# Transposes of the second normalisation moved to the bank of probabilities times values, with their activations split over two steps

## What is computed

```python
x = x + tanh(g_xattn[0]) * xattn(layernorm(x), ctx, ctx, mask, Wq, bq, Wk, bk, Wv, bv)
x = x + tanh(g_ffn[0]) * ffn(layernorm(x), Wg, W1, W2, W3)
# xattn: softmax((q Wq + bq)(k Wk + bk)^T / sqrt(10), masked) (v Wv + bv), by head
# ffn:   scores = (x_flat @ Wg.T).T ; each of 8 experts takes its top n/8 tokens
#        y = (silu(xg W1) * (xg W3)) W2 * softmax(top scores), added back by token
```

## Time and profile before

| | us |
|---|---|
| median of 3 runs | 1004.09 |
| lowest, highest | 1002.74, 1007.72 |
| the profiled execution | 999.87 |
| its span | 998.1 |
| PE busy | 783.9 (79%) |
| DVE busy | 608.9 (61%) |
| ACT busy | 516.7 (52%) |
| POOL busy | 401.4 (40%) |

### The profile page before, as it was taken

The page is one execution under the profiler, slowest core; times in us unless marked ns, Lnnn a source line. Parts: engine busy times, 40 slices in busy tenths (PEclk is TensorE's granted clock), DMA queues, the critical chain, the costliest instruction groups (busy, mean ns, idle before and its releaser), DMA issues. The chain is left out here.

```text
span 998.1 us, 22875 instructions
## 1 busy us (share of the span) xinstructions
PE 783.9 (79%) x7244; PEld 615.0 (62%) x7244; DVE 608.9 (61%) x1501; ACT 516.7 (52%) x1002; POOL 401.4 (40%) x777
## 2 busy tenths in 40 slices
PE   3488888798889888987897721116899999999994
PEld 1366666566666665665666511112798899889884
DVE  1457777677667667766767618879545544644530
ACT  2356576657665666666566711000555665666551
POOL 3344334433443344334432132003355675575434
PEclk9799999999999899989999955555899999999997
DMA  3875558656866585667556235001154365453223
GB/s 116 233 202 129 162 173 237 172 167 178 227 156 180 159 220 148 186 185 184 155 144 159 71 94 186 0 1 44 44 109 119 72 128 113 109 92 47 55 33 42
DMA packets 99261, 130.60 MB, mean 131 GB/s; under 512 B 12896, under 2 KB 62336, under 8 KB 99200
## 3 DMA queue, kind: packets, MB, share of 16 engines
q1 hardware_dynamic: 86912, 112.78, 40.2%
q0 software_dynamic: 12288, 17.05, 10.5%
HBM read 52.34 MB, written 26.49 MB: 79 GB/s over the span
## 5 line engine op out<-in xcount | busy, mean ns | idle before, releaser
L684 DVE TENSOR_REDUCE m_sb<-a_ps 128x4 f32<-128x512 f32 x256 | 165.0, 676 | 17.5 <-PE a_ps L825 16.4
L541 ACT ACTIVATE p_t<-b_ps 128x512 f32<-128x512 f32 x256 | 147.6, 587 | 52.4 <-PE b_ps L838 50.3
L1351 POOL DMA_INDIRECT out<-y,idx_add x64 | 100.1, 1565 | 107.8 <-DVE idx_add L1451 71.6
L825 PE MATMUL a_ps<-k_st,q_st 97*128 97x128 bf16 x1024 | 100.2, 221 | 21.7 <-DMA k_st<-k_part 16.2
L1341 POOL DMA_INDIRECT xg<-rows_scratch,idx x64 | 67.7, 1058 | 103.6 <-issue 89.1
L455 POOL TENSOR_TENSOR q_part<-q_rest,q_part 128x512 bf16<-128x512 f32 x32 | 36.9, 1154 | 179.4 <-ACT q_part L512 179.4
L825 PEld LDWEIGHTS a_ps<-k_st,q_st 97*128 97x128 bf16 x1024 | 73.9, 98 | 55.4 <-issue 48.9
L838 PE MATMUL b_ps<-q_st,k_st 99*128 99x128 bf16 x1024 | 100.2, 221 | 4.7 <-ACT p_t L541 4.7
L1549 PE MATMUL bank<-x_hi,w_hi 128*128 128x512 f32 x256 | 100.7, 393 | 1.5 <-DVE x_lo L1477 1.5
L1549 PE MATMUL bank<-x_hi,w_lo 128*128 128x512 f32 x256 | 99.9, 390 | 0.0
L1549 PE MATMUL bank<-x_lo,w_hi 128*128 128x512 f32 x256 | 99.7, 390 | 0.0
(11 more groups left out here) (193 smaller groups left out, 1728.4 us busy)
## 6 DMA issues: line engine op xcount, KB each, us to landing
q_st<-q_part SPq DMA_DIRECT2D x96, 256.0 KB, 4.7
k_st<-k_part SPq DMA_DIRECT2D x96, 256.0 KB, 4.1
w<-in_w_t SPq DMA_DIRECT2D x24, 512.0 KB, 4.9
rows_scratch<-row SPq DMA_DIRECT2D x16, 528.0 KB, 4.1
x_in<-in_x SPq DMA_DIRECT2D x16, 512.0 KB, 4.9
c_t<-in_ctx_t SPq DMA_DIRECT2D x16, 512.0 KB, 4.9
x_res<-in_x SPq DMA_DIRECT2D x16, 512.0 KB, 3.7
out<-x SPq DMA_DIRECT2D x16, 512.0 KB, 3.3
```

What stands on the lines that cost most here:

```text
L541: act.activation(p_t[b.s % 2][:, 4 * q:4 * q + 4, :], b_ps[q % 2][:].rearrange("p (h s) -> p h s", s=P), ACT.Exp, scale=SCALE).then_inc(ex ...
L684: dve.tensor_reduce(m_sb[b.s % 2][:, 4 * q:4 * q + 4], a_ps[q % 2][:].rearrange("p (h s) -> p h s", s=P), AX_X, ALU.max).then_inc(max_done, 1)
L825: mm = pe.matmul(a_ps[q % 2][:, i * P:(i + 1) * P], q_st[g.p][0:A_K, h, tok], k_st[g.p][0:A_K, h, tok], start=True, stop=True)
L1351: pool.indirect_dma_start(out[:, :], bass.IndirectOffsetOnAxis(ap=idx_add[e.p][:, st:st + 1], axis=0), y[st][:], None, compute_op=ALU.add) ...
```

## The change

- `xn2_back` writes `pv_ps` instead of `o_ps`, half 0 in step 0 and half 1 in step 1, both for group g-3. It waits for the copy of `pv_ps` of batch b-4 (`pv_out`). `values` of that step waits for the copy of the half (`xt2_out`).
- `out_back` has `o_ps` for itself and waits for DVE's last use of it (`ot_out`) alone.
- `normalise2` makes two rows' activations in step 2 and two in step 3, where it made four in step 2.
- `router` and `router_out` are done in step 1 (from 0), `scores_back` and `row_scores` in step 2 (from 1), `store_scores` in step 3 (from 2). `store_rows` stays in step 3, and what it waits for is made a step later.

The diff:

```diff
--- before.py
+++ after.py
@@ -252,25 +252,6 @@
 
 
 
-    O_USES = sorted([((j, OT_AT), "ot", j) for j in range(GB)]
-                    + [((3, 0), "xt", 0), ((0, 0), "xt", 1)])
-    O_LAG = {("xt", 0): 2, ("xt", 1): 3}
-
-    def o_free(eng, g, q, j):
-
-        at = [x[0] for x in O_USES].index((j, q))
-        for back in range(1, 4 * len(O_USES)):
-            i, turn = (at - back) % len(O_USES), (at - back) // len(O_USES)
-            (_, what, n) = O_USES[i]
-            if what == "ot":
-                use = Batch(g.k, 4 * g.p + n + 4 * turn, NB).back(4)
-                if use.ok:
-                    return wait(eng, ot_out, use.times(1, 1))
-            else:
-                use = g.on(turn - O_LAG[what, n])
-                if use.ok:
-                    return wait(eng, xt2_out, use.times(2, n + 1))
-
     with nc.Block() as block:
 
         @block.sync
@@ -394,9 +375,9 @@
                 if b.j == 1:
                     store_x2(g.on(-2))
                 if b.j == 2:
-                    store_scores(g.on(-3))
                     stack_q(g.on(1))
                 if b.j == 3:
+                    store_scores(g.on(-3))
                     store_rows(g.on(-3))
                     stack_k(g.on(1))
                 max_rows(b.back(1))
@@ -565,7 +546,7 @@
                 if g.ok:
                     act.wait_ge(xt2_done, g.times(2, k + 1))
                     wait(act, r_done, g.times(1))
-                    act.activation(xn2_t[:, k, :], o_ps[:], ACT.Copy).then_inc(xt2_out, 1)
+                    act.activation(xn2_t[:, k, :], pv_ps[:], ACT.Copy).then_inc(xt2_out, 1)
 
             def router_out(g):
                 if g.ok:
@@ -599,10 +580,8 @@
                 if b.j == 2:
                     hi_k(f, 0)
                 neg_hi(b.back(1))
-                if b.j == 0:
-                    xt2_copy(g.on(-3), 1)
-                if b.j == 3:
-                    xt2_copy(g.on(-2), 0)
+                if b.j < 2:
+                    xt2_copy(g.on(-3), b.j)
                 if b.j == 2:
                     normalise2(g.on(-2), (0, 1))
                 if b.j == 3:
@@ -619,13 +598,13 @@
                     hi_q(f, 1)
                 if b.j == 2:
                     hi_k(f, 1)
-                if b.j == 2:
+                if b.j == 3:
                     normalise2(g.on(-2), (2, 3))
                 if b.j == 3:
                     normalise(g.on(2), (2, 3))
                 exp(b.back(2), 2)
                 pv_copy(b.back(3))
-                if b.j == 0:
+                if b.j == 1:
                     router_out(g.on(-3))
                 if b.j == 1:
                     mid_q(f, 1)
@@ -765,7 +744,7 @@
                 if b.j == 3:
                     make_v(f, 1)
                 maximum(b, 3)
-                if b.j == 1:
+                if b.j == 2:
                     row_scores(b.group.on(-3))
 
             steps(dve, step)
@@ -839,10 +818,12 @@
                                    start=True, stop=True)
                 mm.then_inc(b_done, 1)
 
-            def values(b, q):
+            def values(b, q, back):
                 if not b.ok:
                     return
                 if q == 0:
+                    if b.j in (1, 2) and back.ok:
+                        pe.wait_ge(xt2_out, back.times(2, b.j))
                     pe.wait_ge(f_free[1], b.group.times(4, 4))
                     pe.wait_ge(f_free[0], b.group.times(4, 4))
                     wait(pe, pv_out, b.times(1))
@@ -882,10 +863,10 @@
                 if use.ok:
                     if isinstance(use.k, int) and use.k + use.s == 0:
                         pe.wait_ge(f_free[1], 4)
-                    if b.j == 1 and g.ok:
+                    if b.j == 2 and g.ok:
                         pe.wait_ge(r_out, g.times(1, 1))
                         pe.sem_inc(passed, 1)
-                    if b.j == 2 and g.ok:
+                    if b.j == 3 and g.ok:
                         pe.wait_ge(st_out, g.times(1, 1))
                     wait(pe, nmid_done, use.times(1))
                     pe.wait_ge(max_done, use.times(4, 4))
@@ -894,18 +875,21 @@
             def out_back(b):
                 use = b.back(4)
                 if use.ok:
-                    o_free(pe, b.group, OT_AT, b.j)
+                    wait(pe, ot_out, use.times(1))
                     pe.wait_ge(pv_out, use.times(1, 1))
                     for a in range(4):
                         mm = pe.transpose(o_ps[:, a * P:(a + 1) * P], o_t[use.s % 2][:, a, :], ident[:])
                     mm.then_inc(ot_done, 1)
 
-            def xn2_back(g, k, at):
-                if g.ok:
-                    o_free(pe, *at)
+            def xn2_back(g, k, b):
+                if g.ok:
+                    last = b.back(4)
+                    pe.wait_ge(pv_out, last.times(1, 1) if last.ok else NB)
+                    if k == 1 and not b.back(3).ok:
+                        pe.wait_ge(xt2_out, g.times(2, 1))
                     pe.wait_ge(xn2_done, g.times(4, 4))
                     for t in range(GB):
-                        mm = pe.transpose(o_ps[:, t * P:(t + 1) * P], row[g.p][:, t, k * P:(k + 1) * P], ident[:])
+                        mm = pe.transpose(pv_ps[:, t * P:(t + 1) * P], row[g.p][:, t, k * P:(k + 1) * P], ident[:])
                     mm.then_inc(xt2_done, 1)
 
             for u in range(8):
@@ -923,19 +907,17 @@
                     scores_t_(*((b.back(2), q - 1) if q else (b.back(3), 3)))
                     if q == 2:
                         for i in range(4):
-                            values(b.back(3), i)
-                        if b.j == 0:
+                            values(b.back(3), i, g.on(-3))
+                        if b.j == 1:
                             router(g.on(-3), b)
-                        if b.j == 1:
+                        if b.j == 2:
                             scores_back(g.on(-3), b)
                     if q in (0, 2):
                         front(g.on(1), 2 * b.j + q // 2)
                     if q == 0:
                         max_t(b)
-                    if (b.j, q) == (3, 0):
-                        xn2_back(g.on(-2), 0, (g, q, b.j))
-                    if (b.j, q) == (0, 0):
-                        xn2_back(g.on(-3), 1, (g, q, b.j))
+                    if q == 0 and b.j < 2:
+                        xn2_back(g.on(-3), b.j, b)
 
             steps(pe, step)
 
```

## The result

The changed kernel is slower: 1012.10 us (median of 7 runs, 1006.65 to 1016.77) against 1004.09, a ratio of 1.0063 with a 95% interval of 1.0040 to 1.0086. The forecast was 1004.0 us, with 995 to 1012 as its range. The profiled execution took 1012.28 us, 12.4 more than that of before. Of these, 8.1 lie in the attention part. The other 4.3 us lie behind it, in code that the change doesn't touch. Over all the traces that part took 411.8 to 416.5 us, and both ends of that range are traces of the kernel before, so they are scatter.

What follows compares the result with a forecast made beforehand. It took POOL's chain and the transfers into `k_st` as the bound, not PE's step 3 waits. Terms 0 - 3.3 + 4.5 - 1.4 = -0.2 us against the profiled 999.87; by the median 1004, range 995 to 1012.

Steps and rivals of the forecast that it cites:

- 2 written-out ones: Written-out groups: the late store of the rows was to cost 0.5 us in each, as in full-clock groups.
- What bounds the kernel: Loop groups at full clock: POOL's chain and the last transfer into `k_st` set the end, not PE's step 3 waits.
- The naive 30 us: Step 3: both PE waits, 2.75 us in each of some 12 groups, counted as saved in full; the forecast rejected this.
- Step 3 at half clock, -3.3 us: Step 3: the 1.1 us gained is kept only in the three loop groups partly at half clock, -3.3 us.
- The moved pieces, 0: Stretch from first scores to last projection of q: moved transposes and router work cancel; 0, bounds -0.3 and +0.4 us a group.
- a wait of 0.2 to 0.3: Same stretch: PE's wait for the copy of half 1, 0.2 to 0.3 us, was to go out of it.
- The store, +4.5 us: Step 3: later store of the rows delays the pieces of k by 0.5 us in nine groups, +4.5 us.
- The clock, the rival at 0.17: First scores: longer PE idle drops the clock, 1.0 to 1.5 us a group, some 1011 us in half of them; chance 0.17.
- The drain, -1.4 us: Last batch: transposes into `o_ps` follow `values` by 1.7 us, not 3.2; -1.4 us, bounds -0.5 and -2.
- The rival of the bubbles: All 12 groups: `k_st` comes earlier along with step 3, so the 1.13 us stay; 989 us, chance 0.05.

Runs made afterwards that it cites:

- the bank alone: Kernel before with only the second normalisation's transposes moved from `o_ps` to `pv_ps`, same steps 3 and 0: 995.32 us, ratio 0.9939.
- the trace without it: Changed kernel with 64 semaphore increments that nobody waits for at the start of PE's program: single run 1006.92 us beside 1004.86.

## Why the prediction was wrong

The step that failed is the price of the written-out groups. The sum has 9 x 0.5 us for the store, of which 1.0 for the "2 written-out ones", and -1.4 for the drain; it has nothing for the clock. Measured, groups 2 and 3 took 5.7 us more: 1.4 for a landing beside PE's program, 1.0 for the store, and 3.2 for half clock behind the waits that these two made. The last stretch took 1.5 more, not 1.4 less. The loop came out near its sum (+0.5 us against -3.3 + 3.5), but by luck: neither of its two terms had the size that was given to it (seven groups at full clock some 0.2 us longer each, three at half clock 0.9 shorter in all).

**What bounds the kernel** held, for its full-clock groups: without both PE waits these took 33.5 us, inside the 33.2 to 33.9 forecast, and the wait for `k_st` rose to 30.4 us, inside the 25 to 35 forecast (the same scores have 13.2 us more under "issue", 5.4 before). The naive 30 us were rightly refused.

**Step 3 at half clock, -3.3 us.** The place was right and the term too small where the clock fell there: with the bank alone such groups take 0.8 us less where the half clock had lasted 3.4 us and 2.3 where it had lasted 6.8, since the half clock itself gets shorter. But in the changed kernel the clock falls behind the first scores instead, in three groups of the loop as in groups 2 and 3, and the loop as a whole came out at +0.5.

**The moved pieces, 0.** Against before this held: the rest of a full-clock group is 14.1 to 14.4 us after and 14.1 to 14.3 before. But the balance hid a gain that the change needn't have given back. With the bank alone the rest is 13.7 to 13.9 us, since "a wait of 0.2 to 0.3" is gone there and no second set of transposes has come into the stretch.

**The store, +4.5 us.** This term failed: its rate does not fit any group. It was worked out on a loop group and taken as 0.5 us for each of nine groups, the "2 written-out ones" too. In the loop it costs 0.1 to 0.2 us. In the written-out groups k is ready 1.5 to 2.1 us earlier, the store at 8.56 us holds SP's queue ahead of it, and issue plus landing come to +1.3 us in group 3 and +2.4 in group 14 (PE's first scores: +1.0 and +1.9, the latter with a packet of PE's program among the pieces; +0.6 in the trace without it). The earlier trace rows are of the loop alone; the same two rows of group 3 or 14 would have shown it.

**The clock, the rival at 0.17.** This is what happened, in a milder form. It was to decide "from an idle time between 2.2 and 3.04 us", from one group. In the changed kernel's loop the clock fell behind 1.71, 1.91 and 1.92 us of idle, while other groups with 1.6 to 1.9 us kept it, and so did group 4 with 2.29. So no length of idle decides it alone, and with the forecast's own 1.7 to 2.2 us of idle in front of exposed work in every group, 0.17 looks too little. Its price of 1.0 to 1.5 us a group was a little low: 1.6 us measured in each of the three.

**Group 2, not in the sum.** The sum has no term for it beyond the store's, and it lost 1.4 us to the landing beside PE's program and 1.6 to the clock.

**The drain, -1.4 us.** Right in its own place and size, though the whole last stretch came out 1.5 us longer: from the last `values` to the last transpose of scores it took 17.96 us before and 16.69 after, -1.3, and the transposes into `o_ps` follow by 1.9 us where I had 1.7. The half clock between the first scores of group 14 and that point took 0.9 us of it back, and the later start of those scores 1.9.

```profile
577.77 1.08 PE L833 MATMUL pv_ps<-p_t,v_aug 128*32 128x128 f32 x32
...
579.66 0.63 PE L881 MATMUL o_ps<-ident,o_t 128*128 128x128 f32 x4 [0.55 <-ACT o_t L535]
```

**The rival of the bubbles.** The rule of the Trainium skill cited there (Perfetto Trace Analysis, section "Matmuls") is that independent matmul groups rotate through PSUM banks. The bank alone agrees with its sign (-0.6%). The way is not the rival's: `k_st` came no earlier, and the wait for it only shrank where the half clock filled it. What stays open is what makes the clock fall in one group and not in its like, why the half clock is shorter with the bank alone, where the split's 4.7 us lie, and why the same PE program has its packet 6 us or 12 us after the issue of k when only SP's order differs.

## What to carry to other kernels

Try the parts of such a change apart: here a freed bank (-6 us) was hidden under three moves of steps (+12 us) that nobody needed for it. Work out a queue's collision on each kind of group, since written-out and looped ones have their transfers ready at other times. And an idle time moved to just before exposed work can cost the clock there, even when it is no longer than the idle times taken away together (here 1.9 us against 2.75).

## What the runs showed of the hardware

PE's program arrives in packets of 16 KB, about 1.2 us of one DMA engine each. In this kernel's written-out groups they come some 4 to 19 us apart; in the loop there are some in its first two groups and its last, and none between. One that fell among six transfers of 256 KB in groups 1 and 2 went with a last landing 5.5 to 6.0 us after its issue instead of 4.4 to 4.5; 64 added instructions moved it by 4 us, 192 by 9. A half-clock stretch of a loop group lasted 3.4 us in some and 6.8 in others. The bank alone has five of them in its loop, before only three, and is the faster: which work a stretch meets, and how long it lasts, counted for more than how many there are.
